# GAT layer on one core: the value products of a head moved from VectorE to GpSimd

## The reference, cut to what matters

```python
seq = (x @ W_seq).reshape(N, H, DH)                 # N = 2048, H = 16, DH = 32
scores = leaky_relu(score1[:, :, None] + score2[:, None, :], 0.2)
scores = scores + (1.0 - adj)[None] * MASK_VAL
attn = softmax(scores, axis=-1)
hidden = einsum('hij,jhd->ihd', attn, seq).reshape(N, D_IN) @ W_out + b_out
x = layernorm(x + elu(hidden))
x = layernorm(x + Coefficient2 @ normalised((adj + adj.T) / 2 + I) @ x)   # Coefficient2 = adj here
```

## Time and profile before

| | |
|---|---|
| median of 3 runs | 750.47 us (750.43 to 752.11) |
| the profiled execution: device time | 751.52 us |
| its span, first to last instruction | 749.7 us |
| TensorE clock granted | 0.998 of full speed |
| busy share of the span | PE 97%, DVE 70%, ACT 55%, POOL 15% |

### The profile page before, as it was taken

The page is one execution under the profiler, slowest core; times in us unless marked ns, Lnnn a source line. Parts: engine busy times, 40 slices in busy tenths (PEclk is TensorE's granted clock), DMA queues, the critical chain, the costliest instruction groups (busy, mean ns, idle before and its releaser), DMA issues.

```text
span 749.7 us, 23470 instructions
## 1 busy us (share of the span) xinstructions
PE 725.1 (97%) x10729; PEld 560.8 (75%) x10729; DVE 528.0 (70%) x891; ACT 409.5 (55%) x315; POOL 114.6 (15%) x141
## 2 busy tenths in 40 slices
PE   4999999999999999999999999999999999999996
PEld 3877899999999999999999996444444444444444
DVE  3457899999999999999999993878741101332332
ACT  1566789898898988989889872423321100000000
POOL 0200000001121311213100001564323100000000
PEclk9999999999999999999999999999999999999999
DMA  8994512413233433335211122896149600011101
GB/s 302 414 361 162 177 41 77 119 59 78 56 71 60 87 75 59 65 67 87 59 36 54 33 73 59 158 195 124 29 70 169 99 1 0 29 43 42 38 33 42
DMA packets 33683, 71.27 MB, mean 95 GB/s; under 512 B 3360, under 2 KB 14240, under 8 KB 31536
## 3 DMA queue, kind: packets, MB, share of 16 engines
q1 hardware_dynamic: 24336, 51.32, 19.9%
q0 software_dynamic: 8416, 17.90, 16.9%
q10 hardware_dynamic: 832, 0.56, 0.2%
HBM read 77.89 MB, written 8.65 MB: 115 GB/s over the span
## 4 chain that ended last, share of the span: by engine, by line
PE 74%; DVE 18%; issue 4%; ACT 1%; DMA 1%; ACTq 0%; DVEq 0%; POOLq 0%; POOL 0%
PE bank L602 14%; PE bank L709 14%; PE bank L695 11%; PE bank L603 8%; PE bank L658 7%; PE bank L544 7%; DVE RZ L1045 6%; PE bank L666 4%; DVE RG L1059 3%; PE bank L608 3%; DVE RG L1055 3%; PE bank L607 3%; PE bank L606 2%; DMA RZ<-in_L_gnn_W_seq_dram 1%; DVE RP L971 1%
## 5 line engine op out<-in xcount | busy, mean ns | idle before, releaser
L602 PE MATMUL bank<-RP,RG 128*128 128x132 f16 (+1 forms) x3072 | 375.8, 221 | 4.9 <-DVE RG L1059 2.6
L603 PE MATMUL bank<-RP,MT 128*128 128x66 f16 (+1 forms) x3072 | 375.2, 196 | 0.0
L788 ACT ACTIVATE RZ<-RZ,TAB 128x2048 int8<-128x2048 f32 x159 | 304.8, 1995 | 20.3 <-DVE RG L1055 20.3
L602 PEld LDWEIGHTS bank<-RP,RG 128*128 128x128 fp8e4 x3072 | 284.7, 98 | 7.1 <-DVE RG L1055 3.0
L603 PEld LDWEIGHTS bank<-RP,MT 128*128 128x128 fp8e4 x3072 | 284.7, 97 | 0.0
L607 PE MATMUL bank<-RP,RG 128*128 128x66 f16 (+1 forms) x1024 | 199.3, 195 | 0.0
L608 PE MATMUL bank<-RP,MT 128*128 128x66 f16 (+1 forms) x1024 | 199.1, 194 | 0.0
L606 PE MATMUL bank<-RP,RG 128*128 128x66 f16 (+1 forms) x1024 | 198.1, 193 | 0.0
L1045 DVE TENSOR_SCALAR RZ<-RZ,TAB 128x2048 int8<-128x2048 f32 x97 | 122.8, 1266 | 0.0
L709 PE MATMUL bank<-RZ,MT 128*128 128x512 f16 (+1 forms) x544 | 110.8, 367 | 0.0
L1055 DVE TENSOR_TENSOR RG<-RZ,MT 128x512 int32<-128x512 int32 x159 | 107.5, 676 | 3.5 <-ACT RZ L788 3.5
(11 more groups left out here) (129 smaller groups left out, 723.2 us busy)
## 6 DMA issues: line engine op xcount, KB each, us to landing
RG<-in_adj_t_dram SPq DMA_DIRECT2D x16, 1024.0 KB, 8.6
RZ<-s_rows_dram SPq DMA_DIRECT2D x60, 256.0 KB, 3.3
seq_copy_dram<-SEQ SPq DMA_DIRECT2D x8, 528.0 KB, 4.9
RZ<-in_x_dram SPq DMA_DIRECT2D x16, 256.0 KB, 3.1
RP<-in_adj_p_dram POOLq DMA_DIRECT2D x8, 512.0 KB, 8.2
RP<-in_adj_tp_dram POOLq DMA_DIRECT2D x8, 512.0 KB, 12.4
out_dram<-W SPq DMA_DIRECT2D x16, 256.0 KB, 2.0
RQ<-in_x_t_dram SPq DMA_DIRECT2D x2, 1024.0 KB, 15.8
```

What stands on the lines that cost most here:

```text
L602: mm(bank[:, c:c + 4 * d], step, both, start=(j == 0 and i % IB == 0), **ends)
L603: last = mm(bank[:, c:c + 4 * d].rearrange("p (e c d) -> p e c d", e=2, c=2)[:, :, 1, :], mask, pn[:, 4:6, :], start=False, **ends)
L788: A(Z[:, m % NZ, :], S1B[u], ACT.Sign, bias=S2[:, h, j:j + 1], scale=-1.0).then_inc(z_ready, 1)
```

## The change

VectorE no longer calls `prep` in attention. `prep(0)`, before the first head, stays on VectorE. For the heads 1 to 15 GpSimd makes the two products, with the same operands and the same counts on `v2_ready`. Its wait for `pn_ready` of h means that `low_operands(h - 1)` is finished, the last reader of V2 of the head before. `low_operands(h - 1)` runs at tile 11 of head h-2, so GpSimd may begin the products of head h there; ScalarE reads them at tile 8 of head h-1. In GpSimd's queue the products of head h stand ahead of the panel transfers of the loop's step h, and its wait for `tabs_done` covers the tables of the heads 8 to 15.

```diff
@@ gpsimd block
+            def prep(h):
+                gp.wait_ge(pn_ready, h)
+                for e, tab in enumerate((EE, FF)):
+                    gp.tensor_tensor(V2[:, :, e, :], SEQ[:, :, h, :], tab[:, h, :].unsqueeze(2).broadcast_to([P, NT, DV]),
+                                     ALU.mult).then_inc(v2_ready, 1)
+
+            prep(1)
             for h in range(2, H):
+                if h == HH:
+                    gp.wait_ge(tabs_done, 2)
+                prep(h)
                 for e in range(NE):
                     if h == 5 + 2 * e:
                         load_pieces(e, h - 1)
@@ vector block, att_tile
                 if h > 0 and j == AT_EVAC + 3:
                     norms(h - 1)
-                if j == AT_PREP and h < H - 1:
-                    prep(h + 1)
                 if j == AT_LOW and h < H - 1:
                     low_operands(h + 1)
```

## The result

The changed kernel takes 759.01 us (median of 4, 758.57 to 759.44) where the kernel before takes 750.59 beside it: ratio 1.0108, 95% interval 1.009 to 1.0125. It is slower by 8.4 us; 7.1 were forecast. The profiled execution takes 758.99 us with a span of 757.2, 7.5 over the one before; that of before lay 0.9 above its median.

A forecast was written before the change was run, and what follows sets the result against it. TensorE was taken to set the pace after 265 us, VectorE before; two 0.95 us stalls a head against 1.24 removed make VectorE the bound: 7.8 less 0.7 gives +7.1, 750.5 to 757.6 us, range 750.9 to 767.

The forecast's parts named there:

- VectorE stands for GpSimd: In attention after tile 11, each GpSimd product holds VectorE for nearly its own length, taken as 0.95 us, twice a head.
- L: VectorE's stall per head from GpSimd's two products: 1.9 us forecast, against 1.24 removed; the change costs nothing at 1.34.
- GpSimd's own time: Length of one 128x528 product on GpSimd: 1.215 us scaled from L437, with 1.06 from L486 as lower end.
- The other signs: In attention, ScalarE's 11.4 us wait for the products gone, and new TensorE waits for L1055 and L1059 in the middle heads.
- 439.0 + 14 L: End of attention in us, from when tile 13 of head 13 is ready; L = 1.9 gives 465.6, 7.8 us later.
- Head 1's pair, costed at nothing: Products of head 1, at about 72 us beside copies out of PSUM: no stall assumed; if wrong, up to 1.9 us more.
- I took off 0.7 us: In 68 to 112 us VectorE idles 3.9 us, so part of the first stall was to fall into that: about 0.7 us less.
- the lead that VectorE had there: At tile 13 of head 13, VectorE finishes the tile 1.4 us before TensorE needs it.
- The cap of 2 to 4 us: In attention TensorE's own 23.25 us a head is a floor, so relieving VectorE gains at most some 2 to 4 us.
- The full-length stall: Rival: in attention VectorE stands for the whole 1.215 us product, L = 2.4, +15, about 765 us; chance 0.13.
- That GpSimd fits in between: Rival: GpSimd runs between VectorE's instructions in attention, L well below 1.24, -2 to -4 us, 747.5; chance 0.10.
- That it can starve: Rival: GpSimd starves behind VectorE's unbroken queue, VectorE loses nothing, result as when GpSimd fits between; included in that 0.10.

The follow-up runs named there:

- `e5_placed_two`: Changed kernel with both GpSimd products released only after tile 8 of the head before, rounding and remainder at tiles 12 and 13: 752.59 us, ratio 1.0012 to the kernel before.
- the placed kernels: Changed kernel with GpSimd's products released after tile 8, rounding and remainder moved back; with both products 752.59 us, or 749.14 with head 1's pair released at once.
- `e10_placed_two_early`: Both GpSimd products released after tile 8, rounding and remainder later, but head 1's pair released at once as in the change: 749.14 us, ratio 0.9964 to the kernel before.

## Why the prediction was right

The mechanism was the one forecast, at every step that decides:

- **VectorE stands for GpSimd.** Two rows after tile 11 are stretched in each head, the two named. Forecast 0.95 each, measured 0.83 and 0.89, L = 1.72 and not 1.9. The step that was mis-sized is GpSimd's own time: 1.215 us from L437, measured 1.07. The lower bound, 1.06 from L486, was the better row: a real second operand costs no more than one element repeated. The other half of the step, the part of the product in which VectorE is free, was taken as 0.30 and is about 0.2. The other signs came too. ScalarE's wait for the products, 11.4 us in the earlier trace rows, is gone, and behind 112 us TensorE has new waits for VectorE (first before, then after: us, times, longest):

```profile
PE bank L602 <- DVE RG L1055: 0.5, 3, 0.2
PE bank L612 <- DVE RG L1065: 5.1, 8, 1.9
```

- **The sum.** Put L = 1.72 in 439.0 + 14 L and attention ends at 463.1 and not 465.6: the size error made the forecast 2.5 us too long.
- **Head 1's pair, costed at nothing, cost 1.1.** VectorE had an own step and a masked tile among the copies out of PSUM, and both stood. Kernel after, in order of time:

```profile
72.06 1.91 DVE L1055 TENSOR_SCALAR RZ<-RZ,TAB 128x2048 int8<-128x2048 f32 x1
73.89 0.41 DVE L910 COPY SEQ<-bank 128x256 f32<-128x256 f32 x1
74.23 0.17 DVE L912 COPY TAB<-bank 128x16 f32<-128x16 f32 x1
74.31 1.15 DVE L1069 TENSOR_TENSOR RG<-RZ,MT 128x512 int32<-128x512 int32 x1
```

  The prediction looked at the copies and not at what stood among them. In this execution the first stage ended 0.47 us earlier, so 0.64 us is left of it at the first tile.

- **The early heads gave nothing back; they took.** I took off 0.7 us because VectorE idles in 68 to 112 us. But it idles there for ScalarE, and ScalarE stood too: its signs wait for VectorE to free their buffers. ScalarE's copy of head 0's sums came 1.1 us later, and VectorE, which had gained 1.24 at tile 4, waited for it. The first row is of the kernel before, the others of the one after:

```profile
112.56 0.27 ACT L779 ACTIVATE RP<-bank 128x132 f32<-128x132 f32 x1
...
113.64 0.27 ACT L789 ACTIVATE RP<-bank 128x132 f32<-128x132 f32 x1
...
113.94 0.98 DVE L999 TENSOR_TENSOR RP<-RP,bank 128x792 f32<-128x792 f32 x1 [0.78 <-ACT RP L789]
```

  At this place the masked tiles go from 0.16 us earlier than before to 0.72 later, 0.88 lost.

- **The account.** At tile 13 of head 13: 14 x 1.72 - 14 x 1.24 = 6.7, + 0.64, + 0.88 makes 8.2 us; measured 8.3. TensorE turned 0.9 of it into nothing, the lead that VectorE had there, forecast as 1.4. Between the two traces 7.5 us were lost where 7.1 were forecast, and that this is so near is luck: the stall, taken 0.18 a head too long, made 2.5 us too much, and the early terms, 2.2 too short, and the lead, 0.5 too long, nearly cancel it. The rest of the 8.4 is that the profiled execution before lay 0.9 above its median.
- **The floor.** The cap of 2 to 4 us for VectorE's relief is shown by the kernel without products, 3.2.
- **The rivals.** The full-length stall is ruled out by the rows: L would be 2.14 with the measured 1.07, and is 1.72. That GpSimd fits in between is ruled out at the change's place. That it can starve was rightly kept open, though not for its reason: the earlier trace rows's 3.1 us are still no proof, but the pair of head 0 in `e5_placed_two` waited some 4 us.
- **One sentence of the prediction was too general:** that GpSimd, coming second, is let in at the end of VectorE's instruction. It holds in the changed kernel in every head. The earlier trace rows could not show it, since no VectorE row that GpSimd holds was next there: L1202 followed, at 519.00, with one input and its usual 0.68 us. In the placed kernels the second product stayed out over several such boundaries.

## What to carry to other kernels

Work taken from a full VectorE and given to GpSimd isn't free for VectorE: where VectorE ran two-input or fast one-input rows, it paid GpSimd's time less 0.2 us. So a product makes VectorE slower if that, here 1.07 - 0.2 = 0.87 us, is more than its own time for it, here 0.62. Place such work beside VectorE's rows with an operand in PSUM, where it was free here, and ask first what the next engine's floor leaves to be gained; here that was 3 us of 750. And list everything that stands between the rows that you call harmless.

## What was not expected of the hardware

- GpSimd's two-input product of 128x528 f32 takes 1.07 us alone, 2.0 ns an element; L437 of 128x1024 took 2.356, 2.3 ns an element, in another access pattern.
- Who gets in when both want to is not settled by "the next boundary". In the changed kernel GpSimd got in at the end of the running VectorE row each time. With the products after tile 8 its second one (at 88.7 us) stayed out while five VectorE rows without a gap went by, 4.2 us, and ran once VectorE was idle; in head 4 of `e10_placed_two_early` it stayed out over two rows and came in behind L1028, where VectorE waits for its own result:

```profile
181.63 0.69 DVE L1071 TENSOR_TENSOR RG<-RZ,MT 128x512 int32<-128x512 int32 x1
182.24 0.70 DVE L1028 TENSOR_TENSOR RP<-RP,TAB 128x528 f32<-128x528 f32 x1
182.97 1.46 DVE L1033 SCALAR_TENSOR_TENSOR RP<-RP 128x528 f32<-128x528 f32 x1
...
180.64 3.23 POOL L478 TENSOR_TENSOR RP<-SEQ,TAB 128x528 f32<-128x528 f32 x2 [21.50 <-DVE RG L1067]
```

  One reading is that a VectorE row that had itself been held gives way at its end, and an unbroken sequence does not. It does not cover the first product of each pair in the changed kernel, which got in behind L1069, a row that nothing had held and that began (at 170.05) before the one in front had ended. What decides was not tried and stays open.
